# A quarter of each diagonal score tile masked by rows of the score stacks, the masking products narrowed to two 64 by 64 triangles

## The reference

```python
q, k, v = split(lora_linear(x, w_attn, b_attn, la_attn, lb_attn))     # [4, 16, 512, 8] each
att = einsum('bhqd,bhkd->bhqk', q, k) / sqrt(8)
att = where(tril(ones((512, 512))), att, -inf)                        # causal
y = einsum('bhqk,bhkd->bhqd', softmax(att), v)
x = layernorm(x + lora_linear(y, w_proj, b_proj, la_proj, lb_proj))
# top-2 routing over 8 experts, expert_out = (silu(x @ gate) * (x @ up)) @ down, weighted sum
x = layernorm(x + ffn(x))
```

## Time and profile before

| | before |
|---|---|
| median of 3 runs | 321.32 us (319.09 to 322.57) |
| the profiled execution | 321.58 us, its span 319.8 us |
| TensorE matmul busy | 254.6 us, 80% |
| VectorE busy | 218.5 us, 68% |
| ScalarE busy | 160.9 us, 50% |
| GpSimd busy | 168.3 us, 53% |
| mean granted TensorE clock | 0.928 |

### The profile page before, as it was taken

The page is one execution under the profiler, slowest core; times in us unless marked ns, Lnnn a source line. Parts: engine busy times, 40 slices in busy tenths (PEclk is TensorE's granted clock), DMA queues, the critical chain, the costliest instruction groups (busy, mean ns, idle before and its releaser), DMA issues.

```text
span 319.8 us, 7232 instructions
## 1 busy us (share of the span) xinstructions
PE 254.6 (80%) x2286; PEld 146.0 (46%) x2287; DVE 218.5 (68%) x576; ACT 160.9 (50%) x275; POOL 168.3 (53%) x301
## 2 busy tenths in 40 slices
PE   4968678889997998979979459974989999999300
PEld 3524323334443343424433137853667867877300
DVE  5559989998989778968928516478254554554870
ACT  4463666667775678667686233521233323333161
POOL 7545665555547577495791711645633433433631
PEclk9969999999999899999997859999899999999855
DMA  6474033330220222232100320113321121117051
GB/s 178 104 206 123 9 102 104 100 102 4 67 70 19 84 86 82 80 91 60 52 1 21 83 53 0 48 46 92 119 92 50 53 67 50 49 45 218 6 162 35
DMA packets 32833, 24.07 MB, mean 75 GB/s; under 512 B 5652, under 2 KB 31735, under 8 KB 32776
## 3 DMA queue, kind: packets, MB, share of 16 engines
q1 hardware_dynamic: 28016, 18.15, 21.1%
q0 software_dynamic: 2624, 4.47, 4.4%
q10 hardware_dynamic: 2160, 1.02, 1.2%
HBM read 10.56 MB, written 6.80 MB: 54 GB/s over the span
## 4 chain that ended last, share of the span: by engine, by line
PE 54%; DVE 23%; issue 7%; ACT 6%; another core or an unknown queue 3%; ACTq 2%; POOL 2%; POOLq 0%; DVEq 0%
PE slot L1589 14%; DVE negm L982 11%; PE pvo L1605 7%; PE pvo L1356 7%; PE slot L1338 4%; PE slot L1597 4%; PE slot L1318 4%; PE slot L1311 3%; PE misc L1364 2%; DVE stats L998 2%; PE misc L1582 1%; ACT Pt L841 1%; ACT rows L819 1%; ACTq L352 1%
## 5 line engine op out<-in xcount | busy, mean ns | idle before, releaser
L982 DVE TENSOR_REDUCE negm<-slot 128x2 f32<-128x1024 f32 (+2 forms) x96 | 96.0, 1041 | 17.4 <-PE slot L1318 17.1
L841 ACT ACTIVATE Pt<-slot 128x1024 f32<-128x1024 f32 (+1 forms) x96 | 81.4, 880 | 40.9 <-PE slot L1338 29.4
L706 POOL DMA_INDIRECT chosen_scratch<-Pt x39 | 38.3, 983 | 61.6 <-ACT Pt L889 56.2
L1589 PE MATMUL slot<-GUW,Pt 128*128 x156 | 55.8, 482 | 0.0
L1356 PE MATMUL pvo<-Pt,V 128*9 128x128 f32 (+3 forms) x512 | 48.4, 451 | 8.8 <-ACT Pt L841 6.9
L587 POOL TENSOR_SCALAR_AFFINE_SELECT Pt<-Pt 128x512 f32<-128x512 f32 x56 | 35.8, 647 | 36.0 <-ACT Pt L841 35.4
L1177 DVE COPY Pt<-slot 128x256 f32<-128x256 f32 x39 | 16.5, 424 | 42.4 <-PE slot L1597 33.7
L889 ACT ACTIVATE Pt<-pvo,Pt 128x128 f32<-128x128 f32 x39 | 14.3, 367 | 55.5 <-PE pvo L1605 35.2
L613 POOL DMA_INDIRECT rows_scratch<-rows,place x32 | 31.6, 989 | 16.0 <-DVE place L1057 8.2
L1338 PE MATMUL slot<-Qs,Ks 64*128 64x512 bf16 (+3 forms) x256 | 32.5, 308 | 8.7 <-DVE negm L982 8.5
L1605 PE MATMUL pvo<-DW,Pt 128*128 (+1 forms) x234 | 33.5, 280 | 1.9 <-issue 1.1
(11 more groups left out here) (224 smaller groups left out, 363.9 us busy)
## 6 DMA issues: line engine op xcount, KB each, us to landing
Pt<-rows_scratch SPq DMA_DIRECT2D x39, 65.0 KB
Qs<-early SPq DMA_DIRECT2D x12, 128.0 KB, 2.5
Qs<-DW SPq DMA_DIRECT2D x12, 128.0 KB, 2.4
Ks<-DW SPq DMA_DIRECT2D x12, 128.0 KB, 2.4
Qs<-chosen_scratch SPq DMA_DIRECT2D x6, 256.0 KB
GUW<-in_L_ffn_gate_proj_dram SPq DMA_DIRECT2D x8, 176.0 KB
GUW<-in_L_ffn_up_proj_dram SPq DMA_DIRECT2D x8, 176.0 KB
Ks<-early SPq DMA_DIRECT2D x9, 128.0 KB, 2.8
```

Of the source, the lines that this page charges most:

```text
L706: pool.indirect_dma_start(chosen_scratch, bass.IndirectOffsetOnAxis(xg[:, ring, C:C + 1].bitcast(U32), 0), ys[:, ring % OUT_RING, :], None ...
L841: act.activation(p_view(g % 2, kb)[:, h0:h0 + heads, :].rearrange("p (c a) q -> p a c q", a=2), t_view(u, k_slot(g, u)), ACT.Exp, scale=SC ...
L982: dve.tensor_reduce(negm[:, g % 2, :, h0 // 2:(h0 + heads) // 2, qb], s_view(u, q_slot(g, u)), AX_X, ALU.max, negate=True).then_inc(max_do ...
L1589: pe.matmul(slot[two][:, w * T:w * T + F], xgT[:, two, :], GUW[:, bass.ds(e, 1), w, :].rearrange("p e f -> p (e f)"), start=True, stop=Tru ...
```

## The change

The upper right quarter of each diagonal tile (queries in the first 64 of a block of 128, keys in the second 64) is masked throughout. The changed kernel puts this into row 7 of each block of the stacks: in `Qs` it is 1 where the token lies in the first half of its 128, in `Ks` -3e38 where it lies in the second half, with one of four blocks of 128 tokens to each of four channel blocks, so that only tokens of the same 128 meet. The mask products keep their number; the first pair covers 64 columns a head instead of 128, in both directions. GpSimd builds the rows in 16 partitions inside `GUW` (one fill of 512 words, then for each of two rows a fill and two selections over 512 elements, on 4 partitions), copies 8 of them to the next 8 partitions by DMA, waits for that in `load_ones`, and issues two more DMAs for each batch (each 16 rows of 8 KB, from pieces of 1 KB). The waits on `ones_loaded` count 64 instead of 32, and SyncE waits for all four before it loads the experts' weights.

```diff
+        hide_rows = up_front[0:2 * D, B * T:B * T + T].bitcast(BF16).rearrange("p (s t) -> p s t", s=2)
...
+        FREE_ROWS_LOADED = 16 * 4
...
             sp.wait_ge(v_out, B)
+            for b in range(B):
+                sp.wait_ge(ones_loaded[b], FREE_ROWS_LOADED)
...
+            def hide_half(row, value, first):
+                pool.memset(row, value).then_inc(hide_ready, 1)
+                hides[0] += 1
+                pool.wait_ge(hide_ready, hides[0])
+                pool.affine_select(out=row, in_=row, compare_op=ALU.is_ge, fill=0.0, base=-first,
+                                   pattern=[[1, T]], channel_multiplier=-P).then_inc(hide_ready, 1)
+                hides[0] += 1
+                pool.wait_ge(hide_ready, hides[0])
+                pool.affine_select(out=row, in_=row, compare_op=ALU.is_ge, fill=0.0, base=first + HALF - 1,
+                                   pattern=[[-1, T]], channel_multiplier=P).then_inc(hide_ready, 1)
+                hides[0] += 1
+
+            hides = [0]
+            pool.memset(hide_rows[:, :, :].bitcast(I32), 0).then_inc(hide_ready, 1)
+            hides[0] += 1
+            pool.wait_ge(hide_ready, hides[0])
+            hide_half(hide_rows[0:TB, 0], 1.0, 0)
+            hide_half(hide_rows[0:TB, 1], NEG, HALF)
+            pool.wait_ge(hide_ready, hides[0])
+            pool.dma_start(hide_rows[D:D + TB], hide_rows[0:TB]).then_inc(hide_copied, 16)
+
             def load_ones(b):
                 pool.wait_ge(ones_ready, 1)
                 pool.wait_ge(cleared[b], 1)
+                pool.wait_ge(hide_copied, 16)
+                for n, stack in enumerate((Qs, Ks)):
+                    pool.dma_start(stack[PRODUCTS + 1:P:BLOCK, QPB * b:QPB * (b + 1)].rearrange("p g c t -> p (g c) t"),
+                                   hide_rows[:, n:n + 1, :].broadcast_to([2 * D, QPB * 2, T])).then_inc(ones_loaded[b], 16)
...
-                    dst, picked, mask = mask_piece(v[:, a, :, qb * P:(qb + 1) * P], half(pick, a)[:, HALF:3 * HALF], half(tri, a))
+                    dst, picked, mask = mask_piece(v[:, a, :, qb * P:qb * P + HALF], half(pick, a)[:, HALF:3 * HALF], half(tri, a)[:, 0:HALF])
...
-                        dst, picked, mask = mask_piece(v[:, a, :, 0:P], half(pick, a)[:, 0:P], half(tri_after, a))
+                        dst, picked, mask = mask_piece(v[:, a, :, HALF:P], half(pick, a)[:, 0:P], half(tri_after, a)[:, HALF:P])
...
-            pe.wait_ge(ones_loaded[0], 32)
+            pe.wait_ge(ones_loaded[0], FREE_ROWS_LOADED)
```

More of the change, by code:

```diff
@@ L124, in causal_attention_then_top2_experts @@
         pick = sb("pick", [P, 3 * HALF], BF16)
+        GUW = sb("GUW", [P, E, 2, F])
+        up_front = GUW[:, 0:E // 2].rearrange("p e w f -> p (e w f)")
         tri = sb("tri", [P, P], BF16)
         tri_after = sb("tri_after", [P, P], BF16)
+        hide_rows = up_front[0:2 * D, B * T:B * T + T].bitcast(BF16).rearrange("p (s t) -> p s t", s=2)
         ones_rows = sb("ones_rows", [PARTS, QPB * 2 * T], BF16)
@@ L227, in causal_attention_then_top2_experts @@
         fill = sb("fill", [P, 2, ROW])
-        GUW = sb("GUW", [P, E, 2, F])
         DW = sb("DW", [P, E, NFC, C])
-        up_front = GUW[:, 0:E // 2].rearrange("p e w f -> p (e w f)")
         up_back = GUW[:, E // 2:E].rearrange("p e w f -> p (e w f)")
@@ L279, in causal_attention_then_top2_experts @@
         cleared = [sem(f"cleared{b}") for b in range(B)]
+        hide_ready, hide_copied = sem("hide_ready"), sem("hide_copied")
         scores_for_max, max_done = sem("scores_for_max"), sem("max_done")
@@ L1565, in _ @@
                     pe.wait_ge(stacks_loaded[(g + 2) // 4], 16 * STACK_DMAS)
-                    pe.wait_ge(ones_loaded[(g + 2) // 4], 32)
+                    pe.wait_ge(ones_loaded[(g + 2) // 4], FREE_ROWS_LOADED)
                 if g == 0:
```

## The result

The changed kernel takes 328.83 us (median of 4 runs, 326.71 to 330.53), the kernel before beside it 320.2: ratio 1.0287, 95% interval 1.0228 to 1.0346. It is about 9 us slower, and above the forecast's range of 318.0 to 325.2. The profiled execution has a span of 326.7 us, against 319.8.

What follows compares the result with a forecast made beforehand. No engine was full over the whole span; VectorE set attention's pace to 70 us, then mostly TensorE. The profiled 321.58 - 1.7 (narrower mask products) + 1.6 (GpSimd's late split) = 321.5 us; range 318.0 to 325.2.

Steps and rivals of the forecast that it cites:

- The step that failed: Start of attention: new copies delay batch 0's K rows by up to about 1 us, counted at nothing.
- the greater of two delays: Start of attention: delays of first scores and of group 0's split do not add; the greater, 1.6 us, counts.
- the split's: GpSimd's split of group 0's maxima: 1.6 us late, about 31.4 instead of 29.76 us; bounds 0 and 6.4.
- (b): GpSimd's queue before group 0's split: slow issues and landing hold the start much longer, about 325 us; chance 0.16.
- GpSimd's sum: GpSimd before group 0's split: 4.3 + 2.6 + 4.5 = 11.4 us of added work against 9.8 us idle.
- Preparation: GpSimd, between mask copies and ones rows: three fills, four selections and waits, 4.3 us; bounds 3.3 and 5.7.
- Small copy: Copy of eight short rows, whose landing the ones rows wait for: 2.6 us; bounds 1.9 and 4.6.
- Issues: GpSimd before group 0's split: six copy issues at 0.75 us each, 4.5 us; bounds 3.2 and 5.9.
- The gain of the narrow products: TensorE's mask products in attention: half as wide first pairs save 1.7 us; bounds 0.3 and 3.9.
- Rival (c): Mask products in attention: the narrower pair brings nothing, waits and weight loads set starts; 322.9 us; chance 0.10.
- TensorE's clock: TensorE at the start: a longer stand lets its clock fall, costing another 1 to 2 us; within (b).

Runs made afterwards that it cites:

- e2: The changed kernel without the two copies for each batch into the stacks, preparation kept, quarter left unmasked; 319.75 us, ratio 1.0001 to the kernel before.
- e1: The changed kernel with the copies reading 128 partitions once, 1 KB each, part of the quarter left unmasked; 322.07 us, ratio 1.0141 to the kernel before.
- e11: As e1, but the copies read 16 partitions standing 8 apart, each 8 times; most of the quarter unmasked; ratio 1.0073 to the kernel before.
- e14: e5 again, on the chip of e15; ratio 0.9931 to the kernel before.
- e5: The kernel before with only the first pair of mask products narrowed, a quarter of each diagonal tile unmasked; ratio 0.9946 to the kernel before.
- e6: The kernel before again, unchanged, for a second trace; 317.4 us.
- e3: The changed kernel with the mask products wide again and hidden rows of -1e37, copies kept; 328.42 us, ratio 1.0294 to the kernel before.
- e8: As e7, but the copies read the change's 16 partitions eight times; 321.15 us, ratio 1.0024 to the kernel before.
- e7: The kernel before with narrow masks from batch 1 on, copies issued later from 128 partitions; 321.02 us, ratio 1.0034 to the kernel before.
- e4: The changed kernel with SyncE issuing the copies into the stacks, batch 0's behind its K rows; 324.98 us, ratio 1.0177 to the kernel before.
- e12: The changed kernel again, on another chip, for a second trace; 315.1 us, ratio 1.0175 to the kernel before.
- e15: e10 again, on the chip of e14; ratio 1.0047 to the kernel before.
- e10: The whole change with rows built early on 64 partitions, copies from 128 partitions, later batches' copies issued behind GpSimd's selections; ratio 0.998 to the kernel before.

## Why the prediction was wrong, point by point

**The step that failed** is, in the prediction's words, "the K rows of batch 0 could land up to about 1 us later (256 KB at about that rate)", counted at nothing. The table of stretches had told that the queues ran at 72 to 76%, and I priced the new bytes at the rate of the old ones. In the change's trace GpSimd's queue ran at 90 to 105 GB/s of engine time (18 to 20 and 16 to 24 us) and took 78% of the engines; SyncE's issues lasted 7.40 instead of 1.90 us, the rows landed after 7.1 instead of 2.6, and the first scores came 6.54 us late instead of 0 to 1. That late start is the copies' doing: without them (e2) it is gone. The upper bound of that term was missing: it had been bounded from the bytes alone. The trace before had a nearer row: the ones rows, which read three neighbouring partitions, moved 0.05 MB in 9.7% of 4 us (26 to 30 us), about 130 GB/s, where the parts ran at 273. The change's description named the source (16 rows of 8 KB from pieces of 1 KB), and I priced only the number of descriptors.

**Who waits on what.** The prediction said that the greater of two delays counts, the first scores' or the split's. That is right, and the one it put at nothing was the greater. GpSimd came out at 30.70 us, 0.94 late instead of 1.6. The sign for (b), a split beyond 34 us, came true (37.17) and would have named the wrong mechanism: the split was late because GpSimd waited for maxima, not because GpSimd was busy.

**The terms of GpSimd's sum.** Preparation: 7.71 to 12.25, 4.54 us against 4.3. Small copy, which goes from partitions 0 to 3 to partitions 8 to 11 and not to the other half of the array: 0.58 and 1.93 until the next issue, 2.5 against 2.6. Issues: 0.54 to 0.58 each, one 0.70, against 0.75; six of them 3.5 us instead of 4.5. By the Trainium skill ("DMA: Bandwidth & Descriptors", on the anatomy of one DMA) many descriptors can be emitted before their cost shows; the trace agrees, 128 pieces at 0.55 us, and the row of 0.81 us that I leaned on was the odd one. With the cheap sources of e1 and e11 this term does come last, but by 0.44 and 0.47 us only.

**The gain of the narrow products** was forecast at 1.7 us and measured at 1.7 (0.8 to 2.6) and 2.2 us (1.3 to 3.1, e14). Rival (c) falls. That it is 1.7 exactly is in part luck: in e5 against e6 steps 1 to 3 shorten by about 0.08 us each instead of 0.1, the later ones by 0.14 at most and 0.08 on average instead of 0.15 to 0.2, and TensorE's busy time in the kernel after falls by 1.1 us (254.6 to 253.5) instead of 2 to 4.

**TensorE's clock** was named only under (b), as 1 to 2 us more behind a longer stand. In the kernel after the stand was 8.19 us, the granted clock 0.50 from 24 to 33 us, and the 6.54 us of the first scores grew to 7.42 at the first transpose: 0.9 us. That the clock alone made them is not shown.

**The size.** 320.2 + 7.4 - 1.7 would be 325.9, 0.7 beyond the range's end and 3 us under the 328.83 measured. On the other chip the same account gives 5.7 us and 5.4 to 5.8 were measured. Rival (b) had the sign, the clock and almost the size (325), by another mechanism; such a loss was held for possible at 0.16 and only through GpSimd.

## What to carry to other kernels

A DMA is priced by its bytes only where its source and destination are spread over the partitions like those of the rows that it is compared with; a copy that reads one small block of neighbouring partitions, as here, is to be built wide first, or issued when nobody needs the queues. Where new transfers enter a stage whose queues are already busy (72 to 76% here), ask who issues there next and who waits for that: the backlog falls on the issues behind it, on the K rows in the change and on the store of the maxima in e3. The late slow copies of e8 cost nothing that the times can tell against the wide ones of e7; the early ones made the first transpose 7 us late. And when two traces are compared, compare the order of the issues first: it moved the first scores by 5.2 us between the change and e3 (with wide masks), which have the same source, and the source by 0.6 between e3 and e1.

## What the runs showed of the hardware

Copies of 0.26 MB that read partitions 0 to 15 eight times took 44.3% of 16 engines for 6 us (98 GB/s, e8); from 128 partitions 15.9% (273 GB/s, e7). In a busier window, 16 to 24 us, where the ones rows are in the sum too, it was 105 GB/s in the change, 214 from 128 partitions (e1) and 233 from 16 partitions 8 apart, read as often (e11). The writes were the same in all of them. The three issues of batch 0's K rows on SyncE took 1.9 to 3.2 us in the traces without early hidden rows or with them behind the K rows (e4), 7.40 and, in e12, 6.00 with the narrow copies issued ahead of them, and 3.25 and 3.70 with wide copies ahead of them (e15, e10). The longest single issue was 3.3 us in the change and 3.5 in e3, against 2.3 in the kernel before. GpSimd's own issues did not lengthen (0.54 to 0.70 us).
